# A third unit of each set transposed by VectorE in 32 x 32 blocks instead of by TensorE, in a graph-attention kernel

## The reference

```
x = layernorm(x + gru_layer(x, adj))          # adj @ x, message, GRU cell
x = layernorm(x + gcn_layer(x, adj))          # normalised adj @ (x @ W)
x = layernorm(x + attention_layer(x, adj))    # below
x = layernorm(x + hyperbolic_layer(x, adj))   # xt = logmap(mobius(x @ W)), adj @ xt, expmap
```

```
q, k, v = x@Wq + bq, x@Wk + bk, x@Wv + bv      # [n, 4, 32]
attn = einsum('nhc,mhc->hnm', q, k) / sqrt(32), -inf where adj == 0
alpha = softmax(attn, axis=-1)
out = einsum('hnm,mhc->hnc', alpha, v)
beta = sigmoid([out, x_r, out - x_r] @ Wb);  out = beta*x_r + (1-beta)*out   # x_r = x@Ws + bs
```

## Time and profile before

| | |
|---|---|
| median of 3 runs | 1848.42 us (1846.78 to 1848.55) |
| profiled execution | 1854.71 us, its span 1852.9 us |
| PE busy | 1764.6 us, 95% of the span |
| DVE busy | 1249.3 us, 67% |
| ACT busy | 959.6 us, 52% |
| POOL busy | 897.4 us, 48% |
| attention stage (first to last attend product) | about 601.3 to 1596.1 us |

### The profile page before, as it was taken

The page is one execution under the profiler, slowest core; times in us unless marked ns, Lnnn a source line. Parts: engine busy times, 40 slices in busy tenths (PEclk is TensorE's granted clock), DMA queues, the critical chain, the costliest instruction groups (busy, mean ns, idle before and its releaser), DMA issues.

```text
span 1852.9 us, 40409 instructions
## 1 busy us (share of the span) xinstructions
PE 1764.6 (95%) x14992; PEld 1163.3 (63%) x14992; DVE 1249.3 (67%) x2454; ACT 959.6 (52%) x1456; POOL 897.4 (48%) x853
## 2 busy tenths in 40 slices
PE   7999999999996999999999999999999999799996
PEld 3444444444444888877878878878778787444442
DVE  4777775222216999998989989979989899201322
ACT  0110110100004989898989978978989899201101
POOL 0111110111126556778687687777786886340111
PEclk9999999999997999999999999999999999899998
DMA  9857666799987555445444555454454543797791
GB/s 374 306 215 264 248 235 240 273 376 379 393 299 244 154 160 162 146 136 162 148 148 144 155 155 149 138 149 143 139 166 148 150 153 105 281 373 283 276 333 65
DMA packets 138525, 396.92 MB, mean 214 GB/s; under 512 B 16240, under 2 KB 67184, under 8 KB 113776
## 3 DMA queue, kind: packets, MB, share of 16 engines
q1 hardware_dynamic: 115776, 353.42, 55.9%
q10 hardware_dynamic: 20016, 32.78, 4.9%
q0 software_dynamic: 2560, 8.39, 1.5%
HBM read 333.19 MB, written 61.34 MB: 213 GB/s over the span
## 4 chain that ended last, share of the span: by engine, by line
PE 73%; POOL 10%; DMA 6%; DVE 4%; issue 3%; SPq 2%; ACT 0%; POOLq 0%; ACTq 0%; DVEq 0%
PE bank L540 32%; PE bank L674 14%; PE bank L647 10%; PE bank L696 9%; POOL arena L1476 3%; POOL small L1483 3%; DMA arena<-group_dram 2%; POOL early L1476 2%; DVE arena L1211 2%; DMA arena<-adj_cols 2%; DMA q_dram<-arena 1%; PE bank L528 1%; SPq L429 1%; PE bank L561 1%; PE bank L562 1%
## 5 line engine op out<-in xcount | busy, mean ns | idle before, releaser
L908 ACT ACTIVATE arena<-arena,small 128x2048 f32<-128x2048 f32 x256 | 512.3, 2001 | 0.0
L674 PE MATMUL bank<-ident,arena 128*128 128x128 f32 x3584 | 477.6, 275 | 0.7 <-ACT arena L908 0.7
L674 PEld LDWEIGHTS bank<-ident,arena 128*128 128x128 f32 x3584 | 423.4, 142 | 66.5 <-issue 3.5
L540 PE MATMUL bank<-arena,stat_s 128*128 128x512 f32 x1008 | 444.7, 598 | 9.7 <-DMA arena<-adj_cols 6.3
L920 ACT ACTIVATE arena<-bank 128x512 f32<-128x512 f32 x624 | 351.1, 596 | 112.4 <-PE bank L674 109.3
L647 PE MATMUL bank<-k,parts 128*128 128x512 f32 x1024 | 375.6, 449 | 13.3 <-DVE small L1211 7.1
L540 PEld LDWEIGHTS bank<-arena,stat_s 128*128 128x128 f32 x1008 | 191.2, 192 | 238.4 <-issue 236.7
L696 PE MATMUL bank<-arena,stat_x 128*32 128x128 f32 x8192 | 280.9, 277 | 27.2 <-DMA arena<-group_dram 27.2
L696 PEld LDWEIGHTS bank<-arena,stat_x 128*32 128x32 f32 x8192 | 207.9, 110 | 85.9 <-issue 48.8
L540 PE MATMUL bank<-arena,stat_x 128*128 128x512 f32 x512 | 230.8, 602 | 10.8 <-DMA arena<-adj_cols 8.5
L1226 DVE COPY arena<-bank 128x512 f32<-128x512 f32 x272 | 181.9, 676 | 44.0 <-PE bank L674 43.9
(11 more groups left out here) (155 smaller groups left out, 1425.7 us busy)
## 6 DMA issues: line engine op xcount, KB each, us to landing
arena<-adj_cols SPq DMA_DIRECT2D x190, 1024.0 KB, 6.4
arena<-adj SPq DMA_DIRECT2D x64, 512.0 KB, 4.8
stat_s<-adj SPq DMA_DIRECT2D x64, 512.0 KB, 4.4
group_dram<-stat_s SPq DMA_DIRECT2D x64, 512.0 KB, 3.0
arena<-group_dram SPq DMA_DIRECT2D x256, 128.0 KB, 2.9
k_dram<-arena ACTq DMA_DIRECT2D x32, 256.0 KB, 6.9
q_dram<-arena ACTq DMA_DIRECT2D x32, 256.0 KB, 11.7
k<-k_dram POOLq DMA_DIRECT2D x32, 256.0 KB, 8.4
```

The costliest lines, as they stand in the source:

```text
L540: mm_ = pe.matmul(bank[:, to, :], stat[:, jt, :], ring[:, s, j, :], start=(jt == 0), stop=(jt == TILES - 1))
L674: last = pe.transpose(bank[:, b_, h * P:(h + 1) * P], cols[:, st % SETS, h, u * P:(u + 1) * P], ident[:, :])
L908: act.activation(cols[:, s_, h, :], cols[:, s_, h, :], ACT.Exp, bias=shift[:, t % 2, 1, i:i + 1], scale=-1.0, accum_out=blocksum[:, t % 2, ...
```

## The change: unit 7 is turned in blocks too

Unit 7 of each set goes the way of units 14 and 15, in a group of its own: group 0 is (7,), group 1 is (14, 15). Each group has its own staging tile, its own place in `group_dram` and its own semaphores. The staging tile of group 0 is chunk 5's part of `stat_s`, and `adj_in[1]` moves to chunks 3 and 4; so xt of chunk 3 goes through memory as well (`SPILLED = (3, 4, 5)`).

In SP's queue the loads of a group now follow directly on its store: store 0, loads 0, mask load, store 1, loads 1, mask load, and behind these the stores of xt, the loads of queries and the store of x3.

DVE turns unit 7 at place 0, unit 14 at place 5 and unit 15 at place 7 (before: 14 at 3, 15 at 5). DVE copies 20 units of a chunk instead of 34, and single exponentials stand at other places.

```diff
-BLOCK_TURN_AT = {14: 3, 15: 5}
-GROUPS = ((14, 15),)
-VECTOR_PLACES = (3, 6)
-VECTOR_ALSO = (8, 12, 25, 27, 29, 33, 48, 58, 60, 61, 66, 75, 85, 87, 89, 90, 91, 105, 106, 109, 116, 120, 122, 124)
-VECTOR_NOT = (6, 22, 35, 67, 115, 118)
-EXP_MOVED = {1: 2, 5: 7, 9: 8, 17: 19, 21: 24, ...}
+BLOCK_TURN_AT = {7: 0, 14: 5, 15: 7}
+GROUPS = ((7,), (14, 15))
+VECTOR_PLACES = ()
+VECTOR_ALSO = (1, 9, 16, 27, 29, 34, 48, 51, 58, 67, 74, 81, 83, 84, 89, 92, 96, 107, 115, 122)
+VECTOR_NOT = ()
+EXP_MOVED = {5: 7, 9: 10, 13: 12, 17: 15, 21: 20, ...}
-SPILLED = (4, 5)
+SPILLED = (3, 4, 5)
...
-        group_blocks = stat_s[:, TILES - 2 * TPC:TILES, :].rearrange("p t f -> p (t f)")
-        adj_in = (arena[:, RING + 4 * CHUNK:RING + 6 * CHUNK], spilled)
+        adj_in = (arena[:, RING + 4 * CHUNK:RING + 6 * CHUNK], spilled[:, 0:2 * CHUNK])
+        tail = stat_s[:, TILES - 2 * TPC:TILES, :].rearrange("p t f -> p (t f)")
+        blocks = [tail if len(group) == 2 else spilled[:, 2 * CHUNK:3 * CHUNK] for group in GROUPS]
...
+            def store_group(g, i):
+
+                n = len(GROUPS[i])
+                sp.wait_ge(blocks_turned[i], n * (g + 1))
+                if g > 0:
+                    sp.wait_ge(group_landed[i], 16 * (P // C) * g)
+                sp.dma_start(group_dram[i, :, 0:n * CHUNK], blocks[i]).then_inc(group_out[i], 16)
+
+            def load_group(g, i):
+
+                n, slots = len(GROUPS[i]), slots_of(i)
+                sp.wait_ge(group_out[i], 16 * (g + 1))
+                if g == 0:
+                    sp.wait_ge(gcn_x2_out, 16 * CHUNKS)
+                if g * UPS + GROUPS[i][-1] >= TURNED:
+                    sp.wait_ge(unit_used, g * UPS + GROUPS[i][-1] - TURNED + 1)
+                for j in range(P // C):
+                    sp.dma_start(slots[j * C:(j + 1) * C, :].rearrange("k (q n) -> k q n", q=P // C),
+                                 group_dram[i, :, j * n * P:(j + 1) * n * P].rearrange("(q k) n -> k q n", q=P // C)
+                                 ).then_inc(group_landed[i], 16)
...
             def attention_loads(c):
                 for st in range(SPC):
-                    for half_set in range(2):
-                        ...
+                    g = c * SPC + st
+                    store_group(g, 0)
+                    load_group(g, 0)
+                    load_mask_ahead(c, 2 * st + 0)
+                    store_group(g, 1)
+                    load_group(g, 1)
+                    load_mask_ahead(c, 2 * st + 1)
+                    if st == 0 and c - 2 in SPILLED:
+                        store_xt(c - 2)
+                    if st % SETS == 1:
+                        ahead = c * TPC + st // SETS + 2
+                        if ahead < CHUNKS * TPC:
+                            load_queries(ahead // TPC, ahead % TPC, False)
+                    if st == 4 and c > 0:
+                        store_x3(c - 1)
                 load_residuals(c)
...
             def load_xt():
                 sp.wait_ge(bias_ready, CHUNKS * COLS)
+                for i in range(len(GROUPS)):
+                    sp.wait_ge(group_out[i], 16 * CHUNKS * SPC)
...
             # mask, DVE
                         dve.wait_ge(unit_turned, pe_turns((c * COLS + m - 3) * UPB))
-                        dve.wait_ge(blocks_turned, block_turns((c * COLS + m - 3) * UPB))
```

More of the change, by code:

```diff
@@ L129, in group_of @@
 def group_of(k):
-    return [group for group in GROUPS if k % UPS in group][0]
+    return [i for i, group in enumerate(GROUPS) if k % UPS in group][0]
 def in_group(k):
-    return group_of(k).index(k % UPS)
+    return GROUPS[group_of(k)].index(k % UPS)
 class TurnBanks:
@@ L280, in group_tiles, with slots_of @@
             return ap.rearrange("p (b u h n) -> p u h b n", b=P // C, u=n, h=H)
-        def slots_of(group):
-            i = group[0] % TURNED - 6
-            return group_slots[:, i * CHUNK:(i + len(group)) * CHUNK]
+        def slots_of(i):
+            first, n = GROUPS[i][0] % TURNED - 6, len(GROUPS[i])
+            return group_slots[:, first * CHUNK:(first + n) * CHUNK]
         def tiles(ap):
@@ L334, in build_program @@
         unit_used = sem("unit_used")
-        blocks_turned = sem("blocks_turned")
-        group_out = sem("group_out")
-        group_landed = sem("group_landed")
+        blocks_turned = [sem(f"blocks_turned{i}") for i in range(len(GROUPS))]
+        group_out = [sem(f"group_out{i}") for i in range(len(GROUPS))]
+        group_landed = [sem(f"group_landed{i}") for i in range(len(GROUPS))]
+        xt_out, xt_in_place = sem("xt_out"), sem("xt_in_place")
         rows_pe, rows_act, rows_dve, rows_pool = [sem(f"rows_{e}") for e in ("pe", "act", "dve", "pool")]
@@ L375, in load_ring @@
                     if first and layer == 2 and s % 4 == 0:
-                        turned_before = (CHUNKS * SPC - 2 + s // 4 + 1) * UPS
-                        sp.wait_ge(unit_turned, pe_turns(turned_before))
-                        sp.wait_ge(blocks_turned, block_turns(turned_before))
+                        sets = CHUNKS * SPC - 2 + s // 4 + 1
+                        sp.wait_ge(unit_turned, pe_turns(sets * UPS))
+                        for i, group in enumerate(GROUPS):
+                            sp.wait_ge(blocks_turned[i], sets * len(group))
                     if not first:
@@ L1580, in factor @@
                     tt("fac", s1, s1, t1, ALU.mult)
-                    if isinstance(c, int) and c == CHUNKS - 2:
-                        pool.wait_ge(group_out, 16 * CHUNKS * SPC * len(GROUPS))
+                    if c == CHUNKS - 2:
+                        for i in range(len(GROUPS)):
+                            pool.wait_ge(group_out[i], 16 * CHUNKS * SPC)
                     to = tiles(mx_g) if c in SPILLED else stat_s[:, c * TPC:(c + 1) * TPC, :]
```

42 lines of the change are left out of this document (14 added, 28 removed).

## The result

The changed kernel takes 1866.98 us in the median of 4 runs (1858.56 to 1873.44), the kernel before, run in turn with it, 1848.49 (1846.78 to 1848.87). The ratio is 1.0092 [1.0068, 1.0117]: about 0.9% slower, where 1808 had been forecast. Its profiled execution took 1865.82 us, span 1864.1; the profiled execution of the kernel before was 6.3 us above its median, so the two profiles lie only 11 us apart where the medians lie 18.5 apart.

A forecast was written before the change was run, and what follows sets the result against it. PE was taken to set the pace in attention. From the profiled 1854.7 us, - 27.8 - 32.8 + 8 + 10 + 2 gave 1814.1, or 1808 for the median (chance 0.50); range 1788 to 1838.

The forecast's parts named there:

- What bounds the kernel: Attention stage: PE sets the pace, busy 119.1 of 119.4 us in the first chunk, DVE and ACT close behind.
- PE's saving: Attention stage: unit 7 no longer turned on PE saves 0.435 us in each of 64 sets, 27.8 us.
- The followers: ACT's and DVE's work in attention: 1 us a chunk lost to them, 8 us in all.
- That rival: ACT becomes the bound in attention: 2 us a chunk more, 1824 us; chance 0.15.
- The late masks: SP's queue at chunk ends: group loads ahead of mask loads end PE's waits, 23.8 + 9 = 32.8 us gained.
- the half clock: PE at 1.2 instead of 2.4 GHz behind its waits in attention: about 9 us lost, counted as gained.
- What is late next: The groups' store and load chains through SP's queue: 0.16 us a set, 10 us in all.
- the margin: Loads of units 14 and 15 against PE's need: 0.5 us after the change, 1 to 2 before.
- groups' chains: Term for both groups' stores and loads: 10 us; as a rival 0.5 us a set, 1830 us, chance 0.16.
- The 2 us at the end of the stage: Before the last layer: one more xt load and a later last store delay the end 2 us.
- The slower one: Long ends of the groups' chains as the rule: loses from 0.79 us a set; at 1.3, 1881 us; chance 0.09.
- not 1 to 3.5 us in pairs but short, if at all: Sign in the new profile: PE's waits for the group's DMA in attention no longer paired, but short or absent.

The follow-up runs named there:

- experiment 4: Experiment 1 with the four loads of queries moved from behind the second group to between the groups: 1818.16 us, ratio 0.9832.
- experiment 2: The kernel before, with only the group's loads put directly behind its store, ahead of the mask load: 1838.46 us, ratio 0.9951.
- experiment 3: The changed kernel with both groups' loads reading adj, so they need not wait for the store (wrong values): 1812.77 us, ratio 0.9803.
- (7): The kernel before, with masks loaded six columns ahead instead of seven: 1831.74 us, ratio 0.9894.
- experiment 10: The kernel before, with the group's loads ahead of the mask load in the last two sets of each chunk only: 1828.74 us, ratio 0.9897.
- experiment 5: The changed kernel with every mask load but the first seven cut from 512 to 256 KB (wrong values): 1820.96 us, ratio 0.9843.
- experiment 1: The changed kernel with the mask load put back between the store and the loads of each group: 1823.76 us, ratio 0.9848.
- experiment 9: Experiment 4 with the loads of units 14 and 15 ahead of the second mask load in each chunk's last two sets: 1819.96 us, ratio 0.9865.
- experiment 8: The changed kernel, with masks loaded six columns ahead instead of seven: 1991.55 us, ratio 1.0738.

## Why the prediction failed

**What bounds the kernel: right.** PE set the pace before, and where SP keeps up it still does: experiment 4's chunk 0 has PE busy for 115.58 of 116.30 us.

**PE's saving, 27.8 us: right for a clean set.** Forecast 0.435 us a set; the group of unit 7 takes 3.45 against 3.88 us, that is 0.43, and a clean set 14.2 where it took 14.7. Over the whole stage PE is busy for 957.0 us in experiment 2 (two units in blocks) and 932.7 in experiment 3 (three), both without half clock: 24.3 us less. It was not all to be had in the sets that wait for something else.

**The followers, 8 us: at most that, and not ACT.** With ACT busy for 93% of chunk 0, PE waits 1.5 us in all for its copies in experiment 3. That rival is out. For DVE's masking PE waits 14.8 us there, 6.8 in experiment 4 and 9.7 in the changed kernel, against 7.1 before.

**The late masks, 32.8 us: the diagnosis right, the size wrong.** The waits of the earlier trace rows do go away with the order. But what stood in the queue behind POOL also gave POOL its masks early. Taken alone the new order gave 10 us (experiment 2), a shorter lead 19 (7), an order for the late sets 18 to 19 (10). "POOL's work doesn't change" was true, but its inputs came later in experiments 2 and 7, and I had taken that nothing else becomes late. That is not all of it: in experiment 10 POOL waits for masks for only 14.6 us, PE's waits for the group are down from 27.2 to 4.6 us, and the half clock in the stage from 22.0 to 1.6 us (by the trace's clock records). There PE's idle time in the stage fell by 16.5 us, not 23.8, and its busy time by 7.6, where I had 9 for the half clock; PE waits 4.1 us for queries instead. That is 24.1 us in the profiles, and 18 to 19 in the medians, since the profiled execution of the kernel before was 6.3 us above its median.

**The failed step: "What is late next", priced at 10 us and about 55 when measured.** I wrote that SP waits for the store to land "with nothing useful in between", and priced this only as latency: is each group back before PE needs it? The time of that wait in SP's queue itself I never summed. Three things were wrong in it.

First the queue's own round. From the records of the changed kernel SP issues for 6.2 us a set, with about 0.5 between the issues, and stands still about 490 / 64 = 7.7 us a set behind its stores. That is 14.4 us, and a clean set is 14.2. It still waits 1.3 us a set for DVE, since the second store can't go before unit 15 is turned, so it can't hide the two halves in each other; the mean round is 15.9.

```
                         stand-still a set   SP's own round   mean round   wait for DVE a set
after                          7.7                14.4            15.9            1.3
experiment 4                   6.1 (*)            12.0            15.2            3.0
half mask (5)                  6.0                12.8            15.2            2.0
(*) with the two mask loads of 0.44 us inside it, counted once in the round
```

The mean round of the last two is that of the chunks, with the work after attention in them; that SP no longer sets it is my reading of its longer waits for DVE.

Then the landing. I took 3.0 us for a store from the earlier trace rows. Those stores went out from a queue that had been waiting for DVE, and at 55 of the 64 no earlier transfer of SP's was in flight any more (in chunk 0 the last mask load was issued at 637.79 and landed at 643.33, the store went out at 646.19). In the changed kernel one was in flight at 127 of 128 stores; a mask load of 512 KB now stands directly in front of 83 of them, and within 1.5 us behind one the same 512 KB store takes 4 to 5 us. With 3.0 us in the sum the round is 6.2 + 0.5 + 2 x 2.6 = 11.9 us (each landing less the 0.4 us of its own issue), which fits; with the 4.0 and 4.3 us (means) measured it is 14.3, which doesn't. A 3.0 read behind an idle queue was used for a busy one.

And the margin. The working took the group's loads as down 4.2 us after the first issue and the margin before the change as 1 to 2 us. In the very set of the earlier trace rows the first load went out at 636.00, but the last of the four landed at 642.34, 6.3 us later, with the next mask load behind it; the 0.30 us in the last line of the earlier trace rows is the wait for it. The margin there was nothing already. The 0.4 us for SP's wake-up was not seen either: 112 of 128 first loads of the changed kernel went out within 0.02 us of the landing.

The Trainium skill (DMA: Bandwidth & Descriptors, "Anatomy of one DMA") gave me an estimate of 2.6 us for the 256 KB store. That section fits transfers issued by GpSimd, and these are issued by SP. The trace comes near the number where no large load stands just ahead (2.4 us in experiment 1, 2.3 in experiment 4) and not in the changed kernel (4.1). That a second group pays the fixed cost twice, which I drew from it, was the right worry; I weighed it for PE's need and not for SP's time.

**The sum.** Forecast for the stage: 994.8 - 27.8 - 32.8 + 8 + 10 = 952.2 us, and 942.2 without the 10 us for the groups' chains. Experiment 3, which leaves the landing out, has 956.4: the other terms together came 14 us short, most of it in the late masks (24.1 in experiment 10's profile for 32.8) and in PE's saving (24.3 for 27.8). The changed kernel has 1011.1, that is 54.7 us more. So the term "groups' chains", 10 us, was about 55. PE's idle time in the stage is 41 of it (65.1 against 24.0 us). The other 14 are busy time (946.3 against 932.7), with 23.9 us of the changed kernel's stage at half clock and 0.2 of experiment 3's; I had forecast none in the middle of the stage. The 2 us at the end of the stage weren't there: from the last attend to the end it took 256.8 us before and 253.9 after.

**The rivals.** The slower one (0.09) named the place, the groups' chains, and its threshold of 0.79 us a set was the right one to ask about: the term has cost 54.7 / 64 = 0.85 us a set. Its trigger was wrong. It counted on DVE's late turn and on landings by chance at their long ends; the landings were long because of where the stores stood. The forecast of waits "not 1 to 3.5 us in pairs but short, if at all" was half right: the pairs are gone, but 24 waits of up to 3.3 us are spread over the stage.

**Open.** The last two sets of a chunk stay long in the versions with three units (about 15 and 16 us in experiment 9, where a clean set takes 14.2); that early and late mask loads trade off there is shown, which order would serve both was not found. Why a store lands later behind a large load is not shown, only that it does. Nor was a second issuing queue for the group tried.

## What to carry to other kernels

Before putting a wait for a landing into a queue that is issued in order, sum that queue's own round: every issue, every stand-still, against the period of the loop that it serves; a latency that fits is not enough. Put an independent transfer between a store and the loads that wait for it, and don't let the store follow a large load. A duration of a transfer holds for the traffic that went ahead of it, so read it from a row with the same neighbours.

## What the hardware showed that I had not expected

- A store issued under 0.2 us behind a 512 KB load on the same queue landed 1.9 us later than one with over 1.5 us between (medians): 5.04 against 3.17 us for 512 KB, 4.58 against 2.62 for 256 KB. Behind a 256 KB load it was 4.09 against 2.62 for 512 KB. A load issued right behind a store does it no such harm (2.9 and 2.4 us in experiment 1). The Trainium skill (DMA: Bandwidth & Descriptors, "Queues, rings and completion order") says that each DMA engine consumes the descriptors of a queue in ring order, so that a store's come behind a load's; the runs agree in kind. An estimate from the rate in "Anatomy of one DMA", 512e3 / 436e3 = 1.2 us, is less than the 1.9 measured.
- It need not be one large transfer: in experiment 1 a 256 KB store right behind the group's four loads of 128 KB landed in 4.75 us (6 stores), right behind the queries' four loads of 64 KB in 2.43 (10). Bytes are not the whole of it: right behind one mask load of 256 KB (experiment 5) the same store took 3.52 us (7). Nor is it traffic in flight as such: in experiment 1 an earlier transfer of SP's was in flight at 95 of the 128 stores, and these had the same median, 2.9 us, as the other 33.
- One column less of lead for the masks cost 125 us in one kernel and gained 19 in another. PE's clock takes part: 143 us of experiment 8's attention stage ran at half clock (1.2 instead of 2.4 GHz), 24 us of the changed kernel's. Of the 131 us by which the stage is longer, 50 are busy time of PE (996.6 against 946.3) and the rest idle time. The mean granted clock was 0.951 and 0.981.
